# Distances of the sampled rows on ScalarE, and a whole third tap group on GpSimd, in a deformable convolution

## The reference, cut to what matters

```python
loc_y = ys + ky + offset[..., 1]
loc_x = xs + kx + offset[..., 0]
sampled = _bilinear_gather(value, loc_y, loc_x)
out = (sampled * mask[..., None]).sum(axis=4)      # over the 9 taps
return out.reshape(N, L, C) @ Wo
```

## Time and profile before

| what | value |
|---|---|
| median of 3 runs | 466.93 us (466.06 to 466.94) |
| the profiled execution's own time | 465.76 us |
| its span, first to last instruction | 464.0 us |
| busy: PE, DVE, ACT, POOL | 86%, 79%, 59%, 36% of the span |
| round 0, from its first sample to its last reduce | about 171 to 249 us |
| round 1, the same | about 264 to 342 us |

### The profile page before, as it was taken

One profiled execution on the slowest core, in us unless ns is written; L12 is line 12 of the kernel. 1 busy time (PEld: TensorE's weight loads), 2 busy tenths in 40 slices (PEclk: granted clock), 3 DMA queues, 4 the chain that ended last, 5 costly groups with the idle time before them and its releaser, 6 DMA issues.

```text
span 464.0 us, 10053 instructions
## 1 busy us (share of the span) xinstructions
PE 399.2 (86%) x4050; PEld 279.2 (60%) x4050; DVE 365.1 (79%) x731; ACT 272.8 (59%) x458; POOL 167.3 (36%) x158
## 2 busy tenths in 40 slices
PE   6988989989887797999878879998788996998775
PEld 5867952223246665666667556666588874554664
DVE  4778888899982577999995779999966866898521
ACT  2742177999905267887742678887412236898240
POOL 5000500000000037899982378999850500000000
PEclk9999999999999799999999999999999996999895
DMA  8300040000032000000000000000000000000000
GB/s 317 131 3 1 1 87 1 2 0 1 1 139 103 1 1 1 2 2 2 1 2 1 1 1 1 2 1 2 2 1 1 1 0 1 2 1 2 1 1 23
DMA packets 1630, 9.89 MB, mean 21 GB/s; under 512 B 208, under 2 KB 976, under 8 KB 1104
## 3 DMA queue, kind: packets, MB, share of 16 engines
q1 hardware_dynamic: 1440, 9.18, 5.5%
q10 hardware_dynamic: 144, 0.07, 0.1%
HBM read 7.99 MB, written 0.26 MB: 18 GB/s over the span
## 4 chain that ended last, share of the span: by engine, by line
DVE 32%; PE 23%; ACT 9%; issue 6%; POOL 2%; DVEq 0%; ACTq 0%; POOLq 0%
DVE SMT L931 8%; DVE PRD L912 6%; DVE wb L912 6%; PE bank L1312 6%; ACT RINGS L605 3%; PE bank L1422 3%; PE bank L1052 2%; PE bank L1402 2%; DVE SMT L923 2%; ACT RINGS L622 1%; PE bank L1197 1%; PE bank L1295 1%; PE bank L1189 1%; ACT RINGS L547 1%; POOL HY L340 1%
## 5 line engine op out<-in xcount | busy, mean ns | idle before, releaser
L1312 PE MATMUL bank<-VB,RINGS 64*128 64x144 f32 x1152 | 95.5, 299 | 18.0 <-DVE wb L912 7.3
L1312 PEld LDWEIGHTS bank<-VB,RINGS 64*128 64x128 f32 x1152 | 76.3, 186 | 43.6 <-issue 19.6
L1052 PE MATMUL bank<-cst 128*128 128x128 f32 x650 | 79.4, 282 | 0.0
L1052 PEld LDWEIGHTS bank<-cst 128*128 128x128 f32 x650 | 78.0, 199 | 0.6
L340 POOL TENSOR_TENSOR HY<-OM,cst 128x324 f32<-128x324 f32 x32 | 23.3, 748 | 121.1 <-DVE LXA L898 121.1
L912 DVE TENSOR_TENSOR PRD<-bank,HY 128x864 f32<-128x864 f32 x48 | 50.3, 1051 | 4.7 <-PE bank L1312 4.1
L912 DVE TENSOR_TENSOR wb<-bank,HY 128x864 f32<-128x864 f32 x48 | 50.4, 1051 | 4.0 <-PE bank L1312 3.4
L547 ACT ACTIVATE RINGS<-bank,cst 128x768 f32<-128x768 f32 x48 | 42.8, 891 | 17.7 <-PE bank L1295 17.6
L550 ACT ACTIVATE RINGS<-RINGS,cst 128x768 f32<-128x768 f32 x48 | 44.9, 936 | 1.6
L1248 PE MATMUL bank<-RINGS,cst 128*32 128x512 f32 x336 | 40.7, 594 | 5.6 <-DVE RINGS L836 2.0
L501 ACT ACTIVATE RINGS<-PRD,wb 128x2048 f32<-128x2048 f32 (+1 forms) x21 | 39.5, 1920 | 5.3 <-PE bank L1248 4.3
(11 more groups left out here) (256 smaller groups left out, 701.2 us busy)
## 6 DMA issues: line engine op xcount, KB each, us to landing
wd<-in_wd SPq DMA_DIRECT2D x1, 2729.5 KB, 10.4
wb<-in_wb SPq DMA_DIRECT2D x1, 2432.5 KB, 10.8
wc<-in_wc SPq DMA_DIRECT2D x1, 1347.0 KB, 13.5
cst<-in_cst SPq DMA_DIRECT2D x1, 765.5 KB, 5.4
PRD<-PRD SPq DMA_DIRECT2D x1, 324.0 KB, 3.5
PRD<-PRD SPq DMA_DIRECT2D x1, 323.9 KB, 4.8
PRD<-PRD SPq DMA_DIRECT2D x1, 323.8 KB, 5.7
XC<-in_x SPq DMA_DIRECT2D x2, 128.0 KB, 2.3
```

The costliest lines, as they stand in the source:

```text
L1052: pe.matmul(bk[:, 0:P], ident, ident, start=True, stop=True)
L1312: ins = pe.matmul(view(bank[q % 2 * 2 + gp], k3 * NR, [[3 * NR, 2 * CG], [1, NR]]), view(HX, b % 2 * HXN + (3 * t + k3) * NPIX + half * P, ...
```

## The change

The line numbers in the profile are those of the kernel before.

- `HY` gets room for all eight images. POOL no longer makes the distances of images 1 to 7; it makes only those of image 0 of a round.
- ACT makes the distances of images 1 to 3 and of 4 to 7 in a new `rows_off`: nine Abs per set, one for each of the nine row numbers, over all images of the set at once (216 and 288 elements each; the output is written with a step of nine elements). `ROWS_AFTER` puts them behind the column hats of images 0, 1 and 2. `rows_hat` loses its own Abs for all images but the first.
- In `last`, POOL adds group 2 of half 0 for all channels (864 elements instead of 432). Half 1 stays as it was.
- DVE needs two reduces for half 0 where there were three: five pieces per image instead of six. `PIECE_AT` puts them behind samples 1 to 5, and none behind sample 0. Every piece of half 0 now waits for the third rise of `paired` of its image (last of half 0), every piece of half 1 for the fourth.
- `PR`, a buffer of the expert layers, now lies in `SM`, which is not in use then. That makes room for the larger `HY`.

```diff
-PIECES = ((0, 0), (0, 1), (1, 0), (1, 1), (0, 2), (1, 2))
+PIECES = ((0, 0), (0, 1), (1, 0), (1, 1), (1, 2))
+PIECE_AT = (1, 2, 3, 4, 5)
+ROWS_AFTER = {(0, 0): (0, 3), (0, 1): (3, 6), (0, 2): (6, 9), (1, 0): (0, 2), (1, 1): (2, 4), (1, 2): (4, 6), (2, 0): (6, 7),
+              (2, 1): (7, 8), (2, 2): (8, 9)}
...
-        PR = sb("PR", 3 * 512)
+        PR = (SM, 0)
...
-        HY = sb("HY", 2 * 2 * HYN)
+        HY = sb("HY", B * 2 * HYN)
...
             def last(turn, b, half):
...
-                second, third = (view(prd(i, half), t * TRIO, [[1, TRIO // GP]]) for t in (1, 2))
+                second, third = (view(prd(i, half), t * TRIO, [[1, TRIO // (GP if half else 1)]]) for t in (1, 2))
                 pool.tensor_tensor(second, second, third, ALU.add).then_inc(paired, 1)
...
                 for b in range(B):
-                    if b + 1 < B:
-                        rows_off(turn, b + 1)
                     pairs(turn, b, 0)
                     if b + 1 < B:
                         masked(turn, b + 1)
...
+            def rows_off(i, rows):
+
+                first, count = ((1, B4 - 1), (B4, B4))[i % B > 0]
+                act.wait_ge(lxa_ready, pointed(i // B, first))
+                for r in range(*rows):
+                    ins = act.activation(view(HY, first * 2 * HYN + r, [[HYN, 2 * count], [NR, 3], [3 * NR, 3 * G]]),
+                                         view(LY, first * 2 * KG, [[KG, 2 * count], [3 * G, 3], [1, 3 * G]]), ACT.Abs, scale=-1.0,
+                                         bias=cv("yg", 1, r))
+                ins.then_inc(hy_abs, 1)
+
             def rows_hat(i):
 
-                hy = view(HY, i % 2 * 2 * HYN, [[1, 2 * HYN]])
-                act.wait_ge(dy_ready, i + 1)
-                act.activation(hy, hy, ACT.Abs).then_inc(hy_abs, 1)
-                act.wait_ge(hy_abs, i + 1)
+                hy = view(HY, i % B * 2 * HYN, [[1, 2 * HYN]])
+                if i % B == 0:
+                    act.wait_ge(dy_ready, i // B + 1)
+                    act.activation(hy, hy, ACT.Abs).then_inc(hy_abs, 1)
+                act.wait_ge(hy_abs, (1 + len(ROWS_AFTER)) * (i // B) + (1 if i % B == 0 else 4 if i % B < B4 else 10))
                 act.activation(hy, hy, ACT.Relu, scale=-1.0, bias=cv("one", 1)).then_inc(hy_ready, 1)
...
             def sums(i, half, part):
...
+                dve.wait_ge(paired, 4 * i + 3 + half)
+                if half == 0 or part == 2:
+                    c = part % 2 * (C // 2)
+                    ins = dve.tensor_reduce(view(SMT, at + c, [[1, C // 2]]),
+                                            view(prd(i, half), TRIO + c * 3 * NR, [[3 * NR, C // 2], [1, 3 * NR]]), AX.X, ALU.add)
+                    if part == 2:
                         ins.then_inc(smp_ready, 1)
                     return
...
                         sample(i, *divmod(u, 2))
-                        if b:
-                            sums(i - 1, *PIECES[u])
+                        if b and u in PIECE_AT:
+                            sums(i - 1, *PIECES[PIECE_AT.index(u)])
```

More of the change, by code:

```diff
@@ L337, in rows_off @@
                 pool.wait_ge(lxa_ready, pointed(turn, b))
-                after(pool, prod_used, IMQ * (i - 1))
                 for half in range(2):
-                    ins = pool.tensor_tensor(by_trio(HY, (b % 2 * 2 + half) * HYN), by_point(LY, 2 * b + half),
+                    ins = pool.tensor_tensor(by_trio(HY, (b * 2 + half) * HYN), by_point(LY, 2 * b + half),
                                              view(cst, CST["yg"], [[0, 3], [0, 3 * G], [1, NR]]), ALU.subtract)
@@ L347, in masked @@
                 for half in range(2):
-                    hy = by_trio(HY, (b % 2 * 2 + half) * HYN)
+                    hy = by_trio(HY, (b * 2 + half) * HYN)
                     ins = pool.tensor_tensor(hy, hy, by_point(MM, 2 * b + half), ALU.mult)
@@ L563, in deform @@
                         rows_hat(i)
[L564 to L570, removed]
+                    for t in range(3):
+                        hats(i, t)
+                        if (b, t) in ROWS_AFTER:
+                            rows_off(i, ROWS_AFTER[b, t])
+                        if t == 0 and b > 1:
+                            rows_hat(i)
+                        if t == 1 and b + 1 < B:
+                            points_out(i + 1)
                     if b == 0:
@@ L913, in sample @@
                                   view(bank[q % 2 * 2], 0, [[512, GP], [6 * NR, CG], [1, 6 * NR]]),
-                                  view(HY, (i % 2 * 2 + half) * HYN + t * 3 * G * NR, [[6 * NR, GP], [0, CG], [1, 6 * NR]]),
+                                  view(HY, (i % B * 2 + half) * HYN + t * 3 * G * NR, [[6 * NR, GP], [0, CG], [1, 6 * NR]]),
                                   ALU.mult).then_inc(prod_used, 1)
@@ L929, in sums @@
                 dve.wait_ge(prod_used, IMQ * i + 5 + half)
-                dve.wait_ge(paired, 4 * i + 1 + half)
                 dve.tensor_reduce(view(SMT, at + c, [[1, C // 4]]),
```

## The result

The changed kernel takes 473.27 us (median of 6 runs, 472.03 to 477.82), the kernel before 466.29 (6 runs, 463.60 to 466.94). The ratio is 1.0168, with a 95% interval of 1.0119 to 1.0216: slower by 5.5 to 10.1 us. The forecast was 469.9, between 467.6 and 472.3. The direction was right, the size was not. The profiled execution has a span of 471.5 us, 7.5 more than before.

The account below looks back on a forecast made before the run. DVE was taken to pace the rounds at 9.03 us per image. Loop 0.66, tail 0.80 and ScalarE's rows 0.05, times two rounds, gave +3.0 on the earlier median of 466.93: 469.9 us, range 467.6 to 472.3.

Parts of the forecast that it names:

- DVE paces the round before: Middle of a round: six samples, six reduces and 0.18 lost fill DVE's 9.03 us per image before the change.
- The loop, 9.14 per image: From s2 through POOL's pairs, mask, pairs, last and DVE's reduce to the next s2: 9.14 for 9.03, +0.66 per round.
- The tail, +0.80: End of a round: DVE's last reduces wait for POOL's longer additions and end at 343.22 against 342.42, +0.80 us.
- Image 1 gains nothing: Start of a round: image 1 gains nothing from its missing reduce, since its s1 waits for PE.
- `PR` in `SM`, and the larger `HY`: Buffer placement: changes no wait, costs nothing.
- ScalarE's rows: New Abs rows in images 0 and 1: 0.28 us per 216 elements, 0.36 per 288, adding 0.05 us per round.
- rival 2: ScalarE late in images 0 and 1 because single-element writes nine apart are dear: 476.7 us in all, chance 0.12.
- the halfway case: ScalarE's rows in images 0 and 1 at r = 0.4 us each: about +2 us, range up to 472.3.
- the doubled one: ScalarE's rows at r = 0.62 us each: +3.8 in round 0, about +3.0 in round 1, +6.8 in all, chance 0.12.
- The sum: Loop, tail and ScalarE's rows over two rounds: (0.66 + 0.80 + 0.05) x 2 = 3.0 us slower.
- Rival 1: Faster: DVE still paces the rounds, an image takes 8.52 us, 459.8 us in all, chance 0.07.
- rival 3: No change: free hand-over between POOL and DVE and a loop of 8.97 us, 467.8 us in all, chance 0.08.

Follow-up runs that it names:

- experiment 3: The changed kernel with the masks one image earlier on POOL, and ScalarE's row hat of the next image behind each image's hats: 467.60 us, ratio to before 1.0067.
- Experiment 8: The kernel of experiment 7 with the old split and six reduces for the last image of a round alone: 462.41 us, ratio to before 0.9927.
- experiment 4: The kernel before with only the POOL and DVE half: longer addition, five reduces, POOL still making all distances: 477.31 us, ratio 1.0272.
- experiment 1: The changed kernel with ScalarE's new rows written side by side instead of nine elements apart (samples weighted wrongly): 469.33 us, ratio to before 1.0106.
- experiment 5: The kernel before, unchanged, profiled a second time: 464.50 us, ratio 0.9988.
- experiment 7: The kernel of experiment 3 with POOL making distances of images 0 to 3 and ScalarE only those of 4 to 7: 465.31 us, ratio to before 0.9995.

## Why the prediction was wrong, point by point

- **DVE paces the round before.** Right. Without the loop (experiment 3) an image in the middle takes the 8.52 that the sum of DVE's own work gave (8.57 on average).
- **The loop, 9.14 per image.** Right in kind, 9.10 measured. The addition took 2.01 and the hand-over to DVE 0.03 (POOL's first last, started at 214.05, ends at 216.06, DVE starts at 216.10), not 0.07. The profile's 0.48 of idle counts from the end of DVE's record; counted by starts, as the forecast does, DVE waits 216.10 - (214.57 + 0.96) = 0.57, where the sum had 0.65. That makes +0.45 per round for the +0.66 of the forecast.
- **The tail, +0.80.** Right, +0.78. Experiment 8 takes it away by the old split (and its six reduces) for that one image.
- **Image 1 gains nothing.** Right: with five reduces and without ScalarE's rows (experiment 4) the heads are 14.86 and 14.99, as before.
- **`PR` in `SM`, and the larger `HY`.** Right as far as the two profiles show: from round 0 to round 1 pass 15.42 us before and 15.41 after, from the end of round 1 to the end of the span 121.6 and 121.4, with clock dips in different places. No run tested it alone.
- **ScalarE's rows: the step that failed.** The term for ScalarE was mis-sized: "for 216 elements, at about 1 us per 1000, 0.36 and 0.28 [...] I add 0.05 per round." Measured: 0.45, and 0.60 for 288 elements, and +2.1 and +1.5 us per head instead of +0.05. With 0.45 and 0.60 the same working gives nearly that: 175.92 + 9 x 0.45 = 180.0 for the first hats of image 1 (PE wants them at 178.95), and second hats at 180.0 + 1.2 = 181.2 instead of 179.13, 2.1 late. So the mechanism stood in the forecast as rival 2, and its size lies between the halfway case (about +2 in both rounds at r = 0.4) and the doubled one (+6.8 at 0.62): the two heads cost 3.65.
- **Two errors made up that price.** The larger is the write step: 0.08 of the 0.17 that were missing for 216 elements, but 0.17 of the 0.25 for 288, and 2.6 of the 3.65 us of the heads (experiment 1). The other was the choice of row, 0.09 and 0.08, and with it the last 1.07 us of the heads. L557 is a Copy without a bias operand. The new rows are Abs with a scale and a bias, and the trace of before had two instructions with both, the Relus L539 and L550:

```profile
214.57 0.84 ACT L539 ACTIVATE HY<-HY,cst 128x648 f32<-128x648 f32 x1
215.32 0.88 ACT L547 ACTIVATE RINGS<-bank,cst 128x768 f32<-128x768 f32 x1
216.23 0.94 ACT L550 ACTIVATE RINGS<-RINGS,cst 128x768 f32<-128x768 f32 x1
217.07 0.36 ACT L530 ACTIVATE RINGS<-bank 96x256 f32<-96x256 f32 x1
```

  By their starts 648 elements take 0.75 and 768 take 0.84, 0.075 per 100. That puts 216 elements at 0.43 and 288 at 0.48, where 0.37 and 0.43 were measured side by side. It errs on the dear side, but it would have shown that nine rows (3.9 us) do not fit into the 3.0 us that ScalarE had to spare. That the function is not what costs, the trace of before shows too: L537 is an Abs without scale and bias, its 648 elements took 0.74, and L539 with both took 0.84 for as many. The records of 288 elements differ by as much, 0.44 for the Copy and 0.52 for the Abs of experiment 1. Which of the two operands costs it, no run tested.
- **The sum.** Middle 0.9, tails 1.55, heads 3.65: 6.1 us by stages on the profiled executions, 7.0 between the medians. The forecast had 1.3, 1.6 and 0.1. So the loop and the tail, forecast at 2.9, came to 2.5, and the term put at 0.1 for the heads was the larger part. Rival 1 (faster) fell, as the first reduce behind s1' did wait, and rival 3 (no change), as the loop took 9.10 and not 8.97. The 0.9 between stages and medians is of the size of the clock's 1.5 (experiment 5).

## What to carry to other kernels

When work moves off the engine that paces a stage, follow the hand-over around: here the saved reduce waited for the longer addition, and the addition's release waited behind that same reduce, so a loop over two engines that are each less busy than before became the pace. Moving one unrelated step (the mask) out of the loop gave the gain in the middle back (8.57 per image) without changing any cost. Price a small instruction by rows of its own form (same operands, scale and bias, same step of the writes), and where it lands in the first images of a pipeline, count how much slack its engine has there, not over the round.

## What the runs showed of the hardware that was not expected

- ScalarE's writes with a step of 4 or more fp32 elements took about 2.1 ns per element by their starts (216 in 0.45, 288 in 0.60), side by side 216 took 0.37 and 288 took 0.43; a step of 2 was nearly free (0.38), 3 lay between (0.41).
- ScalarE's instructions with a scale and a bias took about 0.09 us longer than those without: 0.84 against 0.74 for 648 elements, 0.52 against 0.44 for 288.
- Executions of one kernel differ by where TensorE drops to half its clock: the kernel before ran from 461.35 us at a mean granted clock of 0.975 to 468.26 at 0.957 (29 runs). Beside these, 12 runs of another kernel still left about 1.5 us on either side (experiment 8), while stage lengths in the profile agreed to 0.05 us wherever the clock stayed at its upper level.
- How long the clock stays at its lower level differs between kernels that do the same work in another order (32 us before, 40 in experiments 3 and 7), and by the estimate of experiment 5 it took back most of what experiment 7 had won in its stages. The cause is open.
